# Vision-transformer tower on one core: the transfers of the extra pixel columns are issued by ScalarE instead of SyncE

## The chip, the cores and the metric

The kernel runs on one core of a Trainium2 chip. The metric is the device time of one execution in microseconds (us). A core has TensorE (PE, matrix products and transposes), VectorE (DVE), ScalarE (ACT), GpSimd (POOL) and SyncE (SP), each working through its own list of instructions in order, and 16 DMA engines that move data between memory and on-chip buffers. A transfer is started by an instruction in the list of SP, ACT or POOL. The five lists meet only through semaphores.

## The reference, cut to what matters

```
patches = X.reshape(B, C, 8, 28, 8, 28).transpose(0, 2, 4, 1, 3, 5).reshape(B, 64, 2352)   # X: (128, 3, 224, 224)
tokens  = einsum('bpi,hi->bph', patches, W) + b                      # hidden size 128
h = concatenate([class token, tokens]) * pos_embed                   # 65 tokens for each of 128 images
h = h + attention(layernorm(h))       # gated attention with an exponential moving average (4 filters) as side branch
h = h + ffn(layernorm(h))             # 8 experts, the 1024 best tokens each, gelu, scatter-add
```

The attention layer runs along the images: for one token position the 128 images are the sequence. All of it is float32. The image tensor is 77 MB and is read once.

## The kernel before, in words

**Patch products.** A patch has 3 x 28 x 28 pixels. The kernel puts channel and pixel row on the partitions (`ROWS` = 84) and takes one matrix product for each pixel column. To need fewer products, the last 9 of the 28 pixel columns (`REST`) are laid, in part, on 42 spare partitions (`EXTRA`), so that 18 products work on 126 partitions and one on 84: 19 passes (`PASSES`) for 512 columns of output.

**Chunks.** The images come in chunks of 16 images for one row of patches: 64 chunks, 8 for each row, 4 for each half of the images. A chunk n goes through these steps:
- SP: three loads (`load_chunk`, line 417) from memory into one of three raw buffers (`RING`).
- ACT: stage `C k 0`, `C k 1`, `C k 2` (line 793): three copies of pixel columns from the raw buffer into the planes that TensorE reads.
- POOL: stage `C k 3` (line 576): a copy of the last 9 pixel columns into one of two staging buffers `ST`, at the end of which `staged` is raised. It first waits until the transfers of chunk n-2 have left that buffer (`extras`).
- SP: stage `w k` (line 429, `stage_w`): waits for `staged` and issues two transfers, from 42 partitions of `ST` each to the 42 spare partitions of the planes; their landing raises `extras`.
- SP: stage `W k` (lines 437 to 439): waits for `copied` and `staged`, that is until the raw buffer is free, and issues the three loads of chunk n+3.
- PE: `token_pass` (line 1325). The first pass of a half waits for `copied` and `extras` of the half's four chunks.

**Groups and slots.** The attention works on groups of four token positions. Time is cut into slots; in each the stages of two groups (`a` the younger, `b` the older) and the work on four chunks are woven together in the one order of the list `SLOT`. Every engine walks through that list and executes those stages that it has, in that order. `run(eng, stages)` does this. A part of the list, as written in the kernel:

```python
"w 2", "C 2 1", "L b", "C 2 2", "W 2", "C 3 0", "c a", "Y b", "C 3 3", "w 3", "C 3 1", "d a", "F a", "M b",
"D a", "I a", "C 3 2", "W 3", "v a", "Q b", "R b", "K 1"]
```

The stages that matter here: `T` transposes new tokens (PE line 1356), `P`, `H`, `L`, `F`, `D`, `I`, `Q`, `R` are evaluated by ACT, mostly out of PSUM (`P` line 680 into QKT, `H` line 761, `L` line 680 into O, `F` line 709, `D` lines 716 and 720, `I` lines 725 to 738). `L b` is followed by `Y b` (DVE statistics, then two POOL instructions, lines 500 and 502), and in POOL's list `C 3 3` stands right behind `Y b`. `F a` finishes the filter output ET, and PE's stage `D` (line 1391) reads it. PE puts its token passes between the stages in fixed numbers (`FILL`): 5 after `L`, 1 after `D`, 4 after `I`, 1 after `Q`, and 4 after `T`, which are the first of a half.

There are 15 slots with chunk work. The rest of the kernel, from about 600 us on, holds the last groups, the choice of the tokens of each expert and the experts.

Of the kernel before, what the change touches and what calls it, by code (L numbers as in the profile page):

```python
# [17 lines left out]
def begun(n):  # L18

    return not isinstance(n, int) or n >= 0  # L20
# [15 lines left out]
def vit_tower(nc, x, tok_w, tok_b, cls_token, pos_embed, proj_v_w, proj_v_b, proj_mx_w, proj_mx_b,  # L36
# [10 lines left out]
    B, C, IMG, _ = x.shape  # L47
    SEQ, D = pos_embed.shape
# [5 lines left out]
    HEADS = damping.shape[1]  # L54
    MAXPOS = (rel_pos_w.shape[0] + 1) // 2
    E, _, FF = w1.shape
    FC = FF // 128
    CAP = 1024
# [14 lines left out]
    ROWS = C * PATCH  # L73
    EXTRA = ROWS // 2
    KROWS = ROWS + EXTRA
# [5 lines left out]
    CHUNKS = B // CHUNK  # L81
    CCOL = CHUNK * NP
# [6 lines left out]
    with ctx:  # L89
        def sb(name, shape, dt=F32):  # L90
            return ctx.enter_context(nc.sbuf_tensor(name, shape, dt))

        def count(name, per=1):
            return Count(ctx.enter_context(nc.semaphore(name)), per)
# [6 lines left out]
        ST = flat[:, 2 * PLANEW:2 * PLANEW + STAGEW]\  # L101
# [22 lines left out]
        X = sb("X", [128, 4, D])  # L124
# [47 lines left out]
        def area(rows, half, a, m0=0, m1=NCOL // 2):  # L172
            if a < 2:
                v = PL[rows, half, AREA * a:AREA * a + AREA].rearrange("p (m j r) -> p m j r", j=REST, r=2)
            else:
                v = PL[rows, half, 2 * AREA:PLANEW].rearrange("p (m j r) -> p m j r", j=1, r=2)
            return v[:, m0:m1]
# [98 lines left out]
        pe_pro = count("pe_pro")  # L276
# [6 lines left out]
        staged = count("staged")  # L283
        extras = [count(f"extras{a}", 32) for a in range(2)]
        pe_tok = [count(f"pe_tok{h}") for h in range(2)]
# [62 lines left out]
        def group(row, u):  # L348
            g = 2 * row + 1 + u
            return Group(row, g, u, 4, 4 * g - 3, 1 - u)  # L350
# [8 lines left out]
        def slot(i, u, a, b, tokens, more):  # L359


            keep = []
            for entry in SLOT:
                s, *w = entry.split()
                if s == "K":
                    if tokens and u == 1:
                        keep.append((s, (int(w[0]), i)))
                elif s in "CWw":
                    n = int(w[0])
                    row, half = (i, 1) if u == 0 else (i + 1, 0)  # L370
                    if tokens and (more or u == 0):
                        keep.append((s, (4 * half + n, *(int(v) for v in w[1:]), row)))
                else:
                    gr = a if w[0] == "a" else b
                    if gr:
                        keep.append((s, (gr,)))
            return keep
# [3 lines left out]
        def run(eng, stages, tokens_at=None, last=True):  # L381

            def iteration(i, slots, tokens, more):
                for u, (a, b) in enumerate(slots):
                    for s, w in slot(i, u, a, b, tokens, more):
                        if s in stages:
                            stages[s](*w)
                        if tokens_at and tokens and s not in "KCWw":
                            tokens_at(s, i, a, u)
                    if tokens_at and tokens:  # L390
                        tokens_at("end", i, a, u)

            def pair(i):
                return (group(i - 1, 0), group(i - 2, 1)), (group(i - 1, 1), group(i - 1, 0))
            iteration(0, ((CLS, None), (None, None)), True, True)
            iteration(1, ((group(0, 0), CLS), (group(0, 1), group(0, 0))), True, True)
            for i in range(2, NP - 1):
                iteration(i, pair(i), True, True)
            iteration(NP - 1, pair(NP - 1), True, False)
            if last:  # L400
                iteration(NP, pair(NP), False, False)
                iteration(NP, ((None, group(NP - 1, 1)),), False, False)


        @block.sync
        def _(sp):
            def rows_of(k, hy, c):
                return x[CHUNK * k:CHUNK * k + CHUNK, c, ds(hy * PATCH, PATCH), :].rearrange("b p w -> p b w")

            def raw(n, c):  # L410
                return RAW[PATCH * c:PATCH * c + PATCH, n % RING, :].rearrange("p (b w) -> p b w", b=CHUNK)

            def load_chunk(n):

                if n < CHUNKS * NP:
                    for c in range(C):
                        sp.dma_start(raw(n, c), rows_of(n % CHUNKS, n // CHUNKS, c)).then_inc(load[n % RING].sem, 16)  # L417

            def stage_w(k, hy):

                n = CHUNKS * hy + k
                m0 = CCOL // 2 * (k % 4)
                sp.wait_ge(*staged.done(n))
                if k % 4 == 0 and begun(hy - 1):
                    sp.wait_ge(*pe_tok[k // 4].done(hy - 1))
                if k == 4 and hy == 0:
                    sp.wait_ge(*pe_pro.done(7))
                for a in range(2):
                    sp.dma_start(area(slice(ROWS, KROWS), k // 4, a, m0, m0 + CCOL // 2),  # L429
                                 ST[EXTRA * a:EXTRA * a + EXTRA, n % 2, :, :, :]).then_inc(extras[n % 2].sem, 16)  # L430

            def stage_W(k, hy):

                n = CHUNKS * hy + k
                sp.wait_ge(*copied.done(n))
                sp.wait_ge(*staged.done(n))
                sp.sem_inc(passed_sp.sem, 1)
                load_chunk(n + RING)

            load_chunk(0)  # L440
            sp.dma_start(WN, tok_w).then_inc(w_loaded.sem, 16)
            for n in range(1, RING):
                load_chunk(n)
            for k in range(4):
                stage_w(k, 0)
                stage_W(k, 0)

            def stage_M(gr):
                sp.wait_ge(*dve_M.done(gr.g, 3))
                sp.dma_start(out[:, ds(gr.position, gr.tiles), :], O[:, 0:gr.tiles, :]).then_inc(out_stored.sem, 16)  # L450

            def stage_R(gr):
                sp.wait_ge(*dve_Q.done(gr.g))
                sp.sem_inc(passed_sp.sem, 1)
                sp.dma_start(rows_v[:, ds(gr.position, gr.tiles), 0:D], XR[:, 0:gr.tiles, :]).then_inc(row_stored.sem, 16)

            run(sp, {"w": stage_w, "W": stage_W, "M": stage_M, "R": stage_R}, last=False)


            def load_experts(h, e):  # L460
                sp.dma_start(W1s[:, h, :], w1[ds(e, 1), :, :].rearrange("e d f -> d (e f)")).then_inc(w_in[h].sem, 16)
                sp.dma_start(W2s[:, h, :, :], w2[ds(e, 1), :, :].rearrange("e (c f) d -> f (e c) d", f=128))\
                    .then_inc(w_in[h].sem, 16)

            sp.wait_ge(*pe_tok[0].done(NP - 1))
            sp.wait_ge(*pe_tok[1].done(NP - 1))
            for h in range(2):
                load_experts(h, h)
            for gr in (group(NP - 2, 1), group(NP - 1, 0), group(NP - 1, 1)):
                stage_M(gr)  # L470
                stage_R(gr)


            sp.wait_ge(*pr_ready.done(0))
            sp.dma_start(rows_v[:, :, D:ROW], PR).then_inc(pr_stored.sem, 16)

            for e in range(1, E - 1):
                sp.wait_ge(*pe_y.done(2 * e - 1))
                load_experts(1 - e % 2, e + 1)

            sp.wait_ge(*out_stored.done(LAST))
            sp.wait_ge(*row_stored.done(LAST))
            sp.wait_ge(*pr_stored.done(0))
# [150 lines left out]
        def _(act):  # L634
# [147 lines left out]
            def stage_C(k, piece, hy):  # L782
# [13 lines left out]
                if piece == C - 1:  # L796
                    ins.then_inc(copied.sem, 1)

            for k in range(4):
                for piece in range(C):  # L800
                    stage_C(k, piece, 0)
            run(act, {"C": stage_C, "T": stage_T, "X": stage_X, "E": stage_E, "F": stage_F, "D": stage_D, "I": stage_I,
                      "U": stage_U, "P": stage_P, "H": stage_H, "L": stage_L, "Q": stage_Q, "R": stage_R})


# [803 lines left out]
```

## Time and profile before

| | |
|---|---|
| median of 3 runs | 1052.44 us (1049.9 to 1062.08) |
| the profiled execution, its own time | 1068.15 us |
| its span in the profile | 1066.4 us |
| busy: PE, DVE, ACT, POOL | 754.7, 556.6, 445.9, 397.9 us |
| DMA | 126.31 MB, mean 118 GB/s |
| packets of SP's queue | 116.05 MB, 54.1% of 16 engines' span |
| mean granted TensorE clock | 0.868 |

Busy time is the time in which an engine's instructions ran. The span is from the first to the last instruction of the profiled execution; that execution was slower than the three timed ones. In the page's 40 slices of 26.7 us, the DMA engines are at nine tenths or more of their time up to about 600 us, and far below after that.

### The profile page before, as it was taken

How to read it: one execution, taken by the hardware profiler on the slowest of the kernel's cores; microseconds unless marked ns; L12 is line 12 of the kernel's file. 1: busy time of each engine (PE TensorE's matmuls, PEld its weight loads, DVE VectorE, ACT ScalarE, POOL GpSimd, SP SyncE). 2: the span in 40 equal slices, each digit the busy share in tenths (PEclk: the TensorE clock that was granted, in tenths of full speed). 3: DMA queues.
4: the chain of work that ended last, by engine and by line, in shares of the span. 5: the costliest groups of instructions: out<-in, count | busy, mean ns of one | idle time of the engine just before them, and what ended most of it. 6: DMA issues, size and time to landing. Idle time of an engine off the chain costs nothing.

```text
span 1066.4 us, 9698 instructions
## 1 busy us (share of the span) xinstructions
PE 754.7 (71%) x2872; PEld 405.2 (38%) x2872; DVE 556.6 (52%) x1238; ACT 445.9 (42%) x729; POOL 397.9 (37%) x358
## 2 busy tenths in 40 slices
PE   1155497998879989989999995533214897777950
PEld 0122244444434534544445453422213544444520
DVE  0210155776676757768877777673778232221210
ACT  0534254665655646656666532321450332121410
POOL 1021223333233333323433322171103436677775
PEclk9998898999999989999999998856555698888985
DMA  9699988999999998999999211000010113333332
GB/s 219 129 187 191 186 174 172 195 176 187 184 181 179 196 191 164 192 196 195 194 199 202 69 32 38 10 20 10 11 9 22 32 49 56 54 58 61 58 35 25
DMA packets 134625, 126.31 MB, mean 118 GB/s; under 512 B 16565, under 2 KB 124973, under 8 KB 134445
## 3 DMA queue, kind: packets, MB, share of 16 engines
q1 hardware_dynamic: 120768, 116.05, 54.1%
q0 software_dynamic: 11264, 8.66, 6.3%
q10 hardware_dynamic: 2540, 0.99, 0.5%
q8 instruction: 23, 0.38, 0.2%
q14 instruction: 30, 0.24, 0.1%
HBM read 87.92 MB, written 12.98 MB: 95 GB/s over the span
## 4 chain that ended last, share of the span: by engine, by line
PE 20%; DMA 18%; DVE 17%; POOL 15%; issue 14%; SPq 10%; ACT 4%; ACTq 1%; DVEq 0%; POOLq 0%
DMA XS<-XS 14%; POOL out L616 9%; PE bank L1325 8%; SPq L417 6%; POOL XS L605 4%; SPq L429 4%; DVE Y L949 3%; PE bank L1423 3%; DVE QT L1024 2%; ACT XS L811 2%; DVE stats L899 1%; PE bank L1531 1%; DVE XR L891 1%; DVE ET L955 1%; DMA XS<-in_x 1%
## 5 line engine op out<-in xcount | busy, mean ns | idle before, releaser
L1325 PE MATMUL bank<-XS,WT 126*128 126x512 f32 (+1 forms) x608 | 321.5, 665 | 83.7 <-DMA XS<-XS 83.7
L793 ACT ACTIVATE XS<-XS 84x1152 f32<-84x1152 f32 (+1 forms) x192 | 187.8, 1028 | 40.0 <-DMA XS<-in_x 38.4
L1325 PEld LDWEIGHTS bank<-XS,WT 126*128 126x128 f32 (+1 forms) x608 | 116.1, 200 | 226.5 <-issue 225.8
L576 POOL COPY XS<-XS 84x1152 f32<-84x1152 f32 x64 | 88.9, 1389 | 117.0 <-DMA XS<-XS 99.3
L616 POOL DMA_INDIRECT out<-XS x64 | 100.3, 1567 | 24.7 <-issue 18.6
L605 POOL DMA_INDIRECT XS<-token_rows,XS x64 | 62.2, 972 | 100.5 <-DVE XS L1222 76.0
L949 DVE TENSOR_TENSOR_SCAN Y<-qdec,XT 128x512 f32<-128x512 f32 (+1 forms) x68 | 77.4, 1159 | 12.1 <-ACT XT L680 12.1
L836 ACT ACTIVATE XS<-bank,VT 128x512 f32<-128x512 f32 x64 | 44.0, 688 | 93.8 <-PE bank L1531 68.0
L552 POOL TENSOR_TENSOR QT<-QT,XT 128x512 f32<-128x512 f32 (+1 forms) x17 | 23.7, 1397 | 124.2 <-ACT QT L761 124.2
L1010 DVE SCALAR_TENSOR_TENSOR G<-bank,VT,GT 128x512 f32<-128x512 f32 (+1 forms) x34 | 24.5, 727 | 79.9 <-PE bank L1423 79.4
L955 DVE SCALAR_TENSOR_TENSOR ET<-Y,ema_c,ET 128x512 f32<-128x512 f32 (+1 forms) x68 | 63.6, 935 | 1.8
L1531 PE MATMUL bank<-XS 128*128 128x512 f32 x128 | 64.1, 646 | 0.0
L1541 PE MATMUL bank<-XS 128*128 128x512 f32 x128 | 62.1, 631 | 0.0
L1247 DVE TENSOR_TENSOR XS<-bank,XS 128x512 f32<-128x512 f32 x16 | 11.1, 692 | 90.9 <-PE bank L1550 49.4
L1504 PE MATMUL bank<-XS 128*32 128x64 bf16 x520 | 27.9, 211 | 37.1 <-issue 21.0
L911 DVE SCALAR_TENSOR_TENSOR tokT<-bank,VT 128x512 f32<-128x512 f32 x16 | 17.7, 1104 | 55.0 <-PE bank L1325 55.0
L500 POOL TENSOR_SCALAR rsB<-mvB 128x4 f32<-128x4 f32 (+1 forms) x17 | 14.9, 876 | 80.2 <-DVE mvB L904 80.2
L891 DVE TENSOR_SCALAR XR<-O,mvC,rsC 128x128 f32<-128x128 f32 x65 | 38.5, 854 | 7.7 <-POOL rsC L502 7.7
L500 POOL TENSOR_SCALAR rsA<-mvA 128x4 f32<-128x4 f32 (+1 forms) x17 | 4.0, 233 | 102.7 <-DVE mvA L904 102.6
L680 ACT ACTIVATE XS<-bank 128x512 f32<-128x512 f32 x16 | 9.5, 594 | 74.8 <-PE bank L1522 74.8
L1504 PEld LDWEIGHTS bank<-XS 128*32 128x32 bf16 x520 | 22.4, 108 | 46.0 <-issue 29.9
L891 DVE TENSOR_SCALAR O<-O,mvB,rsB 128x128 f32<-128x128 f32 x65 | 30.3, 528 | 16.1 <-POOL rsB L502 16.1
(228 smaller groups left out, 1269.1 us busy)
## 6 DMA issues: line engine op xcount, KB each, us to landing
XS<-in_x SPq DMA_DIRECT2D x192, 392.0 KB
XS<-XS SPq DMA_DIRECT2D x128, 189.0 KB
out<-O SPq DMA_DIRECT2D x16, 256.0 KB, 10.2
token_rows<-XR SPq DMA_DIRECT2D x16, 256.0 KB, 11.6
XS<-in_L_ffn_W SPq DMA_DIRECT2D x16, 256.0 KB, 3.2
XS<-in_L_tok_W SPq DMA_DIRECT2D x1, 1176.0 KB, 10.1
XS<-token_rows,XS POOLq DMA_INDIRECT x64
out<-XS POOLq DMA_INDIRECT x64
```

Source lines behind the costliest of these rows:

```text
L417: sp.dma_start(raw(n, c), rows_of(n % CHUNKS, n // CHUNKS, c)).then_inc(load[n % RING].sem, 16)
L576: pool.tensor_copy(ST[0:ROWS, n % 2, :, :, :].rearrange("p m j r -> p m r j"), px[:, :, :, PASSES:PATCH])\
L605: pool.indirect_dma_start(out=XG[h][:, k, :], out_offset=None, in_=rows_d, in_offset=bass.IndirectOffsetOnAxis(ap=IDX[:, e, k:k + 1], axis ...
L616: pool.indirect_dma_start(out=out_flat, in_=OW[:, e % 2, k, :], in_offset=None, out_offset=bass.IndirectOffsetOnAxis(ap=IDX[:, e, k:k + 1] ...
L793: ins = act.activation(area(slice(0, ROWS), k // 4, piece, m0, m0 + CCOL // 2).rearrange("p m j r -> p m r j"), px[:, :, :, REST * piece:m ...
L891: last = dve.tensor_scalar(dst(t), src(t), mv[:, gr.parity, t, 0:1], rs[:, gr.parity, t:t + 1], ALU.subtract, ALU.mult)
L949: dve.tensor_tensor_scan(Y[:, h % 2, 0:n], qdec[:, h, 0:n], XT[:, p, 0:n], 0.0, ALU.mult, ALU.add)\
L955: dve.scalar_tensor_tensor(out=ET[:, gr.parity, 0:n], in0=Y[:, h % 2, 0:n], scalar=ema_c[:, h:h + 1], in1=ET[:, gr.parity, 0:n], op0=ALU.m ...
L1325: ins = pe.matmul(TOK[half][:, :], WT[rows, t, :], area(rows, half, t // REST)[:, :, t % REST, :], start=(t == 0), stop=(t == PASSES - 1))
L1504: last = pe.matmul(bank[0][0:32, 0:64], OHh[:, e % 2, s // 2, :, s % 2], OHn[:, e % 2, :, s // 2, :, s % 2], start=(s == 0), stop=(s == SE ...
L1531: pe.matmul(bank[3 + f][:, :], W1s[:, h, 128 * f:128 * f + 128], XGT[:, half, :], start=True, stop=True).then_inc(pe_hid.sem, 1)
L1541: last = pe.matmul(bank[7][:, :], W2s[:, h, f, :], HT[:, half, f, :], start=(f == 0), stop=(f == FC - 1))
```

## The change

`stage_w` leaves SP's list and enters ACT's. Its waits, its two transfers and its semaphores stay as they are, as does the list `SLOT`: ACT meets `w k` where SP met it. Four stages `w` that SP executed before its walk through the list, in turns with `W`, are now executed by ACT in turns with its copies.

```diff
@@ SP
-            def stage_w(k, hy):
-                n = CHUNKS * hy + k
-                m0 = CCOL // 2 * (k % 4)
-                sp.wait_ge(*staged.done(n))
-                if k % 4 == 0 and begun(hy - 1):
-                    sp.wait_ge(*pe_tok[k // 4].done(hy - 1))
-                if k == 4 and hy == 0:
-                    sp.wait_ge(*pe_pro.done(7))
-                for a in range(2):
-                    sp.dma_start(area(slice(ROWS, KROWS), k // 4, a, m0, m0 + CCOL // 2),
-                                 ST[EXTRA * a:EXTRA * a + EXTRA, n % 2, :, :, :]).then_inc(extras[n % 2].sem, 16)
...
             for k in range(4):
-                stage_w(k, 0)
                 stage_W(k, 0)
...
-            run(sp, {"w": stage_w, "W": stage_W, "M": stage_M, "R": stage_R}, last=False)
+            run(sp, {"W": stage_W, "M": stage_M, "R": stage_R}, last=False)
@@ ACT
+            def stage_w(k, hy):
+                n = CHUNKS * hy + k
+                m0 = CCOL // 2 * (k % 4)
+                act.wait_ge(*staged.done(n))
+                if k % 4 == 0 and begun(hy - 1):
+                    act.wait_ge(*pe_tok[k // 4].done(hy - 1))
+                if k == 4 and hy == 0:
+                    act.wait_ge(*pe_pro.done(7))
+                for a in range(2):
+                    act.dma_start(area(slice(ROWS, KROWS), k // 4, a, m0, m0 + CCOL // 2),
+                                 ST[EXTRA * a:EXTRA * a + EXTRA, n % 2, :, :, :]).then_inc(extras[n % 2].sem, 16)
             for k in range(4):
                 for piece in range(C):
                     stage_C(k, piece, 0)
-            run(act, {"C": stage_C, "T": stage_T, ...
+                stage_w(k, 0)
+            run(act, {"C": stage_C, "w": stage_w, "T": stage_T, ...
```

## Rows read from the trace of the kernel before

**Rows 1.** The page, slices of 26.7 us; then groups of instructions by line.

```profile
PE   1155497998879989989999995533214897777950
DMA  9699988999999998999999211000010113333332
L1325 PE MATMUL bank<-XS,WT 126*128 126x512 f32 (+1 forms) x608 | 321.5, 665 | 83.7 <-DMA XS<-XS 83.7
```

**Rows 2.** Chain of waits in order: start us, length us, what; start of a half.

```profile
120.95 11.82 DMA XS<-XS
...
168.65 6.42 PE bank L1325 x8
...
574.26 4.07 PE bank L1325 x8
```

**Rows 3.** The same chain, from the slot at 319 us to the one at 394 us.

```profile
319.44 6.16 PE bank L1325 x8
...
343.02 1.29 POOL XS L576
...
344.33 0.79 SPq L429
...
345.17 10.71 DMA XS<-XS
...
356.12 4.07 PE bank L1325 x8
...
377.07 2.51 SPq L417
...
379.62 2.10 SPq L429
...
381.77 12.07 DMA XS<-XS
```

**Rows 4.** Timeline of ACT: start, length, line, what, [idle before, releaser].

```profile
372.37 0.60 ACT L680 ACTIVATE O<-bank 128x512 f32<-128x512 f32 x1 [2.49 <-PE bank L1440]
372.87 0.47 ACT L793 ACTIVATE XS<-XS 84x128 f32<-84x128 f32 x1
373.92 2.53 ACT L793 ACTIVATE XS<-XS 84x1152 f32<-84x1152 f32 x2 [0.59 <-DMA XS<-in_x]
376.79 0.63 ACT L709 ACTIVATE ET<-ET 128x512 f32<-128x512 f32 x1 [0.34 <-DVE ET L955]
```

**Rows 5.** Timeline of POOL in the same slot.

```profile
368.59 1.77 POOL L576 COPY XS<-XS 84x1152 f32<-84x1152 f32 x1
375.05 0.93 POOL L500 TENSOR_SCALAR rsB<-mvB 128x4 f32<-128x4 f32 x1 [4.70 <-DVE mvB L904]
377.61 1.28 POOL L576 COPY XS<-XS 84x1152 f32<-84x1152 f32 x1
```

**Rows 6.** Timeline of PE: stage D and the end of stage T, twice.

```profile
377.47 1.13 PE L1391 MATMUL bank<-ET,WmT 128*128 128x512 f32 x2 [0.34 <-ACT ET L709]
...
388.99 0.60 PE L1356 MATMUL bank<-ident,tokT 128*128 128x128 f32 x4
...
607.56 4.00 PE L1325 MATMUL bank<-XS,WT 126*128 126x512 f32 x8
```

**Rows 7.** Busy time by stretch; the last three columns are granted clock, DMA share, GB/s.

```profile
314.00:316.00 2.00, 0.69 (x7) 0.45 (x5) 1.68 (x4) 1.58 (x3) 0.00 (x0) 1.00 0.99 189
316.00:318.00 2.00, 0.00 (x0) 0.00 (x0) 1.41 (x9) 2.00 (x9) 0.72 (x2) 0.84 0.88 252
322.00:324.00 2.00, 2.00 (x4) 0.82 (x3) 0.00 (x0) 0.00 (x0) 0.28 (x1) 0.50 1.00 167
...
527.10:562.90 35.80, 33.46 (x115) 17.04 (x114) 27.70 (x59) 22.81 (x36) 12.96 (x12) 1.00 0.96 197
```

**Rows 8.** One line: durations of SP's issue of the moved transfers; one of ACT's issues.

```profile
L429 SPq DMA_DIRECT2D XS<-XS x128: 746/791/3780, 15.9 to 597.9; - x128
L646 ACTq DMA_DIRECT2D ema_in<-in_L_attn_damping_factor x1: 1917/1917/1917, 7.3 to 7.3; - x1
L646 ACTq DMA_DIRECT2D ema_in<-in_L_attn_ema_expansion x1: 454/454/454, 9.8 to 9.8; - x1
```

**Rows 9.** The page, transfers by issue: KB each, us from issue to landing.

```profile
XS<-in_L_ffn_W SPq DMA_DIRECT2D x16, 256.0 KB, 3.2
```

More of the change, by code:

```diff
@@ L801, in _ @@
                     stage_C(k, piece, 0)
-            run(act, {"C": stage_C, "T": stage_T, "X": stage_X, "E": stage_E, "F": stage_F, "D": stage_D, "I": stage_I,
+                stage_w(k, 0)
+            run(act, {"C": stage_C, "w": stage_w, "T": stage_T, "X": stage_X, "E": stage_E, "F": stage_F, "D": stage_D, "I": stage_I,
                       "U": stage_U, "P": stage_P, "H": stage_H, "L": stage_L, "Q": stage_Q, "R": stage_R})
```

## The prediction

> **What bounds the kernel now.** I read the page first. Up to about 600 us both TensorE and the DMA engines are in their nines, so this is the part that the change touches; behind it no chunk is moved [rows 1]. The costliest group of PE, the token passes, sat idle for 83.7 us behind the moved transfers [rows 1]. Then the chain of waits in order of time. Between the first passes of a half at 168.65 and 574.26 us lie 11 slots, so a slot is 36.87 us long [rows 2]. One slot in detail: from the first passes at 356.12 us the groups' work leads to POOL's copy `C 3 3`, which ends at 377.61 + 1.28 = 378.89 us, 22.8 us later [rows 3, 5]. SP issues `w 3`, its transfers take 10.7 to 12.1 us to land, and the next first passes start [rows 3]. From the end of `C 3 3` that second leg takes 11.8 us in one slot (344.31 to 356.12) and 15 us in the next (378.89 to 394), where SP had been held by an issue of 2.51 us for a load [rows 3]. So a slot is a cycle of two legs, 22.8 us and about 14 us, and the landing of `w 3` is most of the second.
>
> PE itself is close behind. The last chunk slot, with no loads left, shows what the cycle is without a late landing: 607.56 - 574.26 = 33.3 us [rows 2, 6]. The DMA engines are the other neighbour: 0.96 of a slot of 35.8 us is 34.4 us of transfers [rows 7].
>
> **What the change takes away.** SP no longer issues 128 transfers of 0.79 us median [rows 8]: SP is not what a slot waits for in other places, so this alone is worth nothing; the loads behind them start a little earlier, and their cover is the DMA engines' own backlog. On a queue of its own `w 3` need not stand behind loads. No row shows such a transfer on ACT's queue beside loads. The bounds are 3.2 us, a 256 KB load with the queues nearly empty [rows 9], and today's 12.1 us [rows 3]. I take about 5 us, nearer the short end since the payload of the two is alike; within a slot it will turn out not to matter.
>
> **What it adds to ACT.** In each slot ACT executes four `w`, each a wait for POOL and two issues. The price of an issue on ACT is between 0.45 us and 1.92 us, both from ACT's own queue at the start, the long one while SP was loading [rows 8]. I take 0.79 us, the median of the very same transfers on SP, so 1.6 us for a `w`, 6.4 us a slot. ACT is busy 22.8 of 36 us [rows 7], so the time is there; the order is the trouble, since ACT executes in order.
> - `w 0` to `w 2` find POOL's copy done or nearly done. `w 0` delays `P b` by about 0.5 us and `w 1` delays `H b` by about 1 us. At `w 2` ACT arrives about 370.0, POOL's `C 2 3` ends at 370.4 [rows 5] and 1 us later by the delay of `H b`, so ACT leaves at 373.0 and, after `C 2 1`, starts `L b` at 374.3 in place of 372.37 [rows 4]. PE's result is there earlier. Behind `L b` come DVE's statistics, then POOL's `Y b`, then `C 3 3`. DVE would have been busy for 0.5 us anyway. So the first leg grows by 1.5 us, to 24.3 us, and `C 3 3` ends at 380.4.
> - `w 3` is the dear one. Behind it in ACT's list stand `C 3 1` and `F a`; behind `F a`, on PE, stage `D` and everything up to the next `T`. Today `F a` starts at 376.79, before `C 3 3` has even begun [rows 4, 5]. ACT reaches `w 3` at about 376.7 us, waits until 380.4, issues until 382.0, copies `C 3 1` until 383.3, and only then does `F a`, until 383.9. PE, which had 0.34 us idle before `D` [rows 6], gets about 6 us.
> - From the start of `D` to the end of `T` PE needs 389.59 - 377.47 = 12.1 us; 12.0 us is taken for the fastest [rows 6]. So the second leg becomes 1.6 (issues) + 1.3 (`C 3 1`) + 0.65 (`F a`) + 12.0 = 15.55 us, and the landing of `w 3`, whether 3 or 12 us after 382.0, lies beside it.
>
> Cycle: 24.3 + 15.55 = 39.85 us.
>
> **The clock.** In this trace an idle stretch of PE of 4.7 us, before 319.44, is followed by a fall of the granted clock from 1.00 to 0.50, that is from 2.4 to 1.2 GHz, and it stays there past 324 us [rows 7]. The first eight pass matmuls take 6.16 us then and 4.07 us otherwise, 2.1 us more [rows 3]. An idle stretch of 6 us before every `D` should do the same each time; what follows `D` is nearly all PE. So 41.95 us for the slot, and 41.95 - 36.87 = 5.1 us over today, whose mean already holds such falls.
>
> The Trainium skill, page "DMA: Bandwidth & Descriptors", section "Issuing engines are not separate DMA queues", says that transfers started by ACT, SP or POOL run on the same 16 engines and that another issuer saves only the sequencer's time. By that rule the transfers themselves bring nothing and the sum stays at the ACT delays, which is what I forecast; no row of before can show two issuers' transfers in a slot.
>
> **The sum.** Thirteen slots (132.8 to 607.6 us) have a group `a` and a `w 3`: 13 x 5.1 = +66 us. In the filling of the pipeline, before it, no `F a` of weight is late, and the landing at 120.95 us, 11.82 us long, is on the chain [rows 2]; on a queue of its own it may shorten to 3.2 us: -8.6 us. Together +58 us. The profiled execution would then take 1068 + 58 = 1126 us; it was 1.5% above the median of the runs, so for the median 1052.4 + 58 = 1110 us.
>
> **Rivals.**
> 1. Issues on ACT are dearer, since they are held as SP's are when loads are queued (2.51 us for a load, 2.10 us for the first of `w 3` [rows 3]). The first issue of each `w` then costs 2.1 in place of 0.79 us: 1.3 x 4 = 5.2 us more a slot, all in the cycle, +68 us: about 1178 us. For it: the 1.92 us on ACT's queue [rows 8]; against: in the slots, ACT's own queue holds only these transfers.
> 2. Faster. If transfers on a second queue pass the queued loads and ACT's waits are absorbed, the late landing goes and the cycle falls towards 33.3 us, or the 34.4 us of the DMA engines: 13 x (36.87 - 34.4) = 32 us, with the 8.6 us of the start 41 us less: 1012 us. The Trainium skill, page "DMA: Bandwidth & Descriptors", section "Queues, rings and completion order", says that each DMA engine goes round the queues that have work; that is the passing itself. It decides if `F a` isn't late by more than the 2.5 us that PE now loses a slot to late landings. Against: `F a` starts within 0.34 us of its operand and PE within 0.34 us of `F a` [rows 4, 6], so there is no slack, and `C 3 3` ends 2.1 us after the start of `F a`.
> 3. No change: the clock doesn't fall, an issue on ACT costs 0.45 us, and the delay of `L b` nearly vanishes. The cycle is 39.85 - 0.7 - 1 = 38.1 us, +1.3 us a slot, and 13 x 1.3 - 8.6 = +8 us: 1060 us.
> 4. No fall of the clock alone: 13 x 3.0 - 8.6 = +30 us, 1082 us.
>
> **How the numbers follow.** Forecast 0.50, rival 1 0.17, rival 4 0.16, rival 3 0.08, rival 2 0.09. The range from 1058 to 1170 us takes in rivals 3 and 4 and most of the way to rival 1. Less than 1% (10.5 us) is what a measurement of this kernel can't tell from no change: faster 0.09, same 0.08, slower 0.83.
>
> **What would show it.** Right: ACT's waits list POOL's line 576 with 3 to 5 us in most of 15 slots; PE's largest wait in the slots is that of stage `D` for `F a`, 5 to 7 us each, and the one for the moved transfers is nearly gone; the DMA share of a slot falls to about 0.83; the clock is at 0.50 behind each `D`; first passes of halves are about 42 us apart. The forecast is wrong if `F a` still starts before `C 3 3` has ended, or if slots are under 37 us. Rival 1 shows as a median issue well over 0.79 us on ACT's queue.

## The result, and the profile after

The changed kernel takes 1122.0 us (median of 4 runs, 1119.38 to 1125.85) against 1057.26 us of the kernel before (4 runs of the same comparison): ratio 1.059, 95% interval 1.054 to 1.064. The forecast was 1110 us, range 1058 to 1170, from slots that grow by 5.1 us. The profiled execution spans 1117.9 us, against 1066.4 us before. Medians here and below are of all runs, ratios of the fast ones alone, and the profile of experiment 6 is of a slow execution, so that its slots are not compared.

The page of the changed kernel, which answers to [rows 1]: granted clock and DMA share in tenths by slices, then costliest groups (busy, mean ns | idle before, releaser), then two kinds of transfers.

```profile
PEclk9688689889989989988988989775655598888985
DMA  9799999789789789789789611000010113333433
...
L1325 PE MATMUL bank<-XS,WT 126*128 126x512 f32 (+1 forms) x608 | 317.7, 659 | 40.1 <-DMA XS<-XS 40.0
...
L1391 PE MATMUL bank<-ET,WmT 128*128 128x512 f32 (+1 forms) x34 | 33.0, 1074 | 99.6 <-ACT ET L695 99.5
...
XS<-in_x SPq DMA_DIRECT2D x192, 392.0 KB
XS<-XS ACTq DMA_DIRECT2D x128, 189.0 KB
```

The wait of PE has changed its place. Before, PE sat idle for 83.7 us ahead of its passes, behind the moved transfers, and `D` (line 1391) was no large group. Now it is idle for 99.5 us ahead of `D`, behind `F a` (ACT, line 695), and what is left behind the transfers, 40.0 us in two waits, is in the filling of the pipeline. In the 12 slots that are compared below, the first kind falls from 30.1 us to nothing and the second grows from 4.0 to 68.7 us. The DMA engines, nearly all in their nines before, show a 7 in every third slice from the 14th on.

Waits in total (us, times, longest), of ACT and of PE in the changed kernel:

```profile
ACT XS L779 <- issue: 131.6, 45, 5.5
```
```profile
PE bank L1391 <- ACT ET L695: 99.5, 16, 12.0
PE bank L1325 <- DMA XS<-XS: 40.0, 2, 25.3
```

The 131.6 us before ACT's chunk copies (line 779) are called "issue", since the activation behind a `w` waits for nothing itself: ACT's list stood in the wait for POOL and in the two issues ahead of it. So the row to read for a wait of ACT's queue is the idle time of the next activation. In the slot below it is 5.47 us behind `w 3`: 3.8 us from the end of the last copy (354.62) to the end of POOL's (358.45), then the two issues.

One slot by the chain of waits of the changed kernel, in order of time; it answers to [rows 3] and has no DMA in it:

```profile
357.19 1.26 POOL XS L562
358.48 0.76 ACTq L795
...
359.28 0.76 ACTq L795
...
361.29 0.61 ACT ET L695
...
361.95 2.08 PE bank L1391 x2
364.02 1.71 PE bank L1394 x2
...
368.88 3.84 PE bank L1325 x8
```

PE's timeline of the same slot (start, length, instructions, [idle before, releaser]), against [rows 6]: first passes, `D`, `T`, next first passes.

```profile
335.16 4.00 PE L1325 MATMUL bank<-XS,WT 126*128 126x512 f32 x8
...
361.95 2.08 PE L1391 MATMUL bank<-ET,WmT 128*128 128x512 f32 x2 [5.64 <-ACT ET L695]
...
375.74 0.60 PE L1356 MATMUL bank<-ident,tokT 128*128 128x128 f32 x4
376.17 4.00 PE L1325 MATMUL bank<-XS,WT 126*128 126x512 f32 x8
```

The slot is 376.17 - 335.16 = 41.0 us long. `D` starts after 5.64 us of idle time, and its first two matmuls take 2.08 us, not 1.13 as in [rows 6]. The granted clock of this place, in the third column from the end of each line:

```profile
356.00:358.00 2.00, 0.31 (x1) 0.00 (x0) 1.07 (x2) 0.00 (x0) 2.00 (x2) 1.00 0.88 178
358.00:360.00 2.00, 0.00 (x0) 0.00 (x0) 1.97 (x5) 0.00 (x0) 0.45 (x1) 0.97 0.96 180
360.00:362.00 2.00, 0.05 (x1) 0.05 (x1) 1.79 (x9) 1.81 (x2) 0.00 (x0) 0.50 1.03 194
364.00:366.00 2.00, 2.00 (x4) 0.83 (x3) 1.77 (x4) 0.92 (x2) 0.95 (x1) 0.50 1.01 207
```

### The profile page after: what moved, and what is told of

It is laid out like the page before. It is cut to its first block, busy times and chain, and to the rows that moved or that the text cites. A ratio compares the mean times of both kernels' runs of the same rounds, so it can differ in the third digit from the quotient of the medians.

```text
span 1117.9 us, 9698 instructions
## 1 busy us (share of the span) xinstructions
PE 770.5 (69%) x2872; PEld 410.4 (37%) x2872; DVE 558.6 (50%) x1238; ACT 445.9 (40%) x729; POOL 395.5 (35%) x358
## 4 chain that ended last, share of the span: by engine, by line
PE 27%; POOL 20%; issue 20%; DVE 12%; DMA 7%; ACT 5%; ACTq 5%; SPq 3%; POOLq 0%; DVEq 0%
PE bank L1325 9%; POOL out L602 8%; POOL XS L562 5%; DMA XS<-in_x 4%; ACTq L795 4%; POOL XS L591 3%; PE bank L1391 3%; SPq L417 3%; DVE stats L899 3%; PE bank L1394 2%; ACT XS L811 2%; PE bank L1408 2%; PE bank L1454 1%; POOL rsA L488 1%; DVE XR L891 1%
## 5 line engine op out<-in xcount | busy, mean ns | idle before, releaser
L1325 PE MATMUL bank<-XS,WT 126*128 126x512 f32 (+1 forms) x608 | 317.7, 659 | 40.1 <-DMA XS<-XS 40.0
L779 ACT ACTIVATE XS<-XS 84x1152 f32<-84x1152 f32 (+1 forms) x192 | 193.3, 1031 | 171.1 <-issue 131.6
L1391 PE MATMUL bank<-ET,WmT 128*128 128x512 f32 (+1 forms) x34 | 33.0, 1074 | 99.6 <-ACT ET L695 99.5
L985 DVE TENSOR_TENSOR S<-bank,relb 128x512 f32<-128x512 f32 (+1 forms) x17 | 11.3, 667 | 91.6 <-PE bank L1408 91.6
L1247 DVE TENSOR_TENSOR XS<-bank,XS 128x512 f32<-128x512 f32 x16 | 11.1, 692 | 90.1 <-PE bank L1550 80.4
L1391 PEld LDWEIGHTS bank<-ET,WmT 128*128 128x128 f32 x34 | 8.3, 304 | 114.3 <-ACT ET L695 114.3
L891 DVE TENSOR_SCALAR XR<-O,mvC,rsC 128x128 f32<-128x128 f32 x65 | 40.9, 891 | 8.4 <-POOL rsC L488 8.4
```

Source lines behind the costliest of these rows:

```text
L779: ins = act.activation(area(slice(0, ROWS), k // 4, piece, m0, m0 + CCOL // 2).rearrange("p m j r -> p m r j"), px[:, :, :, REST * piece:m ...
L891: last = dve.tensor_scalar(dst(t), src(t), mv[:, gr.parity, t, 0:1], rs[:, gr.parity, t:t + 1], ALU.subtract, ALU.mult)
L1325: ins = pe.matmul(TOK[half][:, :], WT[rows, t, :], area(rows, half, t // REST)[:, :, t % REST, :], start=(t == 0), stop=(t == PASSES - 1))
L1391: pe.matmul(DB0[:, 0:n], WmT[:, 1, :], et, start=True, stop=True).then_inc(pe_D.sem, 1)
```

## The experiments

Slots are measured from the first passes behind `T` on PE's timeline, over the 12 slots that end at 607.56 us in the kernel before and at 663.06 us in the changed one: 36.58 us and 41.06 us a slot (the 36.58 hold the last slot of 33.3 us). Ratios are of the timed runs to the kernel before on the same chip, whose median there is 1057.3 us for the changed kernel, 1062.2 us for experiments 1 to 4, 1060.9 us for 5 to 8 and 1061.1 us for 9 and 10.

| | median us | ratio, 95% interval | mean of 12 slots, us |
|---|---|---|---|
| changed kernel | 1122.0 | 1.059, 1.054 to 1.064 | 41.06 |
| 1: w 3 behind F a | 1055.0 | 0.989, 0.982 to 0.996 | 36.33 |
| 2: w 3 alone on SP | 1063.7 | 0.999, 0.994 to 1.003 | 36.55 |
| 3: w 3 alone on ACT | 1119.2 | 1.051, 1.044 to 1.058 | 40.74 |
| 4: ACT waits, SP issues | 1095.2 | 1.028, 1.021 to 1.035 | 38.62 |
| 5: four passes moved before D | 1104.2 | 1.044, 1.038 to 1.051 | 39.18 |
| 6: SP issues, w 3 ahead of W 2 | 1046.2 | 0.989, 0.983 to 0.995 | not compared |
| 7: POOL issues | 1051.2 | 0.993, 0.989 to 0.998 | 35.38 |
| 8: w 2 and w 3 behind | 1054.3 | 0.995, 0.991 to 0.999 | 35.54 |
| 9: as 7, loads earlier | 1051.3 | 0.993, 0.989 to 0.998 | 35.84 |
| 10: as 6, loads earlier | 1052.8 | 0.989, 0.984 to 0.994 | 35.90 |

**1. The order alone.** The theory says that ACT's place in the order costs, not the queue. So ACT keeps all 128 transfers, and one entry of the list moves.

```diff
-"C 3 3", "w 3", "C 3 1", "d a", "F a", "M b",
+"C 3 3", "C 3 1", "d a", "F a", "w 3", "M b",
```

> The changed kernel, with w 3 standing behind F a in the list of the slot, and nothing else moved; ACT still issues all 128 transfers. Theory (ACT's order: F a waits behind w 3, which waits for POOL): F a starts about 4.5 us earlier, as soon as DVE is done; w 3 now delays the two evaluations of stage D by about 1.5 us instead. PE's idle time before D falls from 5.6 us to under 1.5 us, the clock doesn't fall there, and the slot goes from 41.0 to about 35.5 us: 12 x -5.5 = -66 us against the changed kernel, median about 1050 us. Rival (a second queue slows the loads, or the 6.2 us of issues in a slot are what ACT lacks): the slot stays at 39 to 41 us, median 1100 to 1122 us.

Measured: 1055.0 us, ratio 0.989. The whole loss is gone, with one entry moved by three places. ACT's timeline in this kernel:

```profile
337.30 2.91 ACT L779 ACTIVATE XS<-XS 84x128 f32<-84x128 f32 x3
340.77 0.63 ACT L695 ACTIVATE ET<-ET 128x512 f32<-128x512 f32 x1 [0.57 <-DVE ET L955]
342.90 1.56 ACTq L795 DMA_DIRECT2D XS<-XS  x2
344.56 0.69 ACT L702 ACTIVATE QKT<-bank,VT 128x512 f32<-128x512 f32 x1 [3.16 <-issue]
```

`F a` starts when DVE is done, and `w 3` now holds the first evaluation of `D` (line 702), after which PE is idle for 0.90 us. This slot, from 319.60 to 354.58 us, takes 34.98 us, as expected. But the mean is 36.33 us. In the other slots another wait comes last; this is the next slot's chain in the same kernel:

```profile
361.04 13.68 DMA XS<-in_x
374.74 2.51 ACT XS L779 x2
377.25 0.51 ACT ET L695
```

`C 3 0` waits for its load, and that again stands ahead of `F a`. The rivals (a slower second queue, or the sum of the issues) are out: both are the same as in the changed kernel.

**2 and 3. Which of the four w.** The two halves of the change: `stage_w` stands in both lists and returns at once for the other's share. For experiment 2 (in experiment 3 the two conditions are exchanged):

```diff
@@ SP, stage_w
+                if k % 4 != 3:
+                    return
...
@@ ACT, stage_w
+                if k % 4 == 3:
+                    return
```

> The changed kernel with w 3 alone given back to SP; w 0 to w 2 stay on ACT. Theory: F a no longer waits for POOL, the idle time before D goes; the late landing of w 3 behind the loads in SP's queue comes back as the end of the slot. Slots of 36 to 37.5 us, median 1050 to 1070 us. Rival (issues on ACT cost by their number, 3 of 4 remain): three quarters of the loss stay, median about 1105 us.

> The other half: w 3 alone on ACT, w 0 to w 2 issued by SP as before. Theory: nearly the whole loss stays; only the delay of L b by w 0 to w 2, about 1.1 us a slot, goes. Slots of about 39.9 us, median about 1109 us. Rival (cost by the number of issues): a quarter of the loss stays, median about 1073 us.

Measured: 36.55 and 40.74 us a slot. With `w 3` on SP nothing is left of the loss. With `w 3` alone on ACT, 40.74 - 36.58 = 4.2 of the 4.5 us are there. One quarter of the transfers makes nine tenths of the loss of a slot. The expected 39.9 us were too low: `w 0` to `w 2` on ACT cost only 0.3 us a slot, not 1.1. A chain of experiment 2 shows the old end of the slot come back (the passes are line 1343 there):

```profile
304.79 10.90 DMA XS<-XS
...
315.94 5.56 PE bank L1343 x8
```

**4. The wait without the issues.** SP issues everything; ACT only waits where `w` stands.

```diff
@@ ACT, stage_w (SP's stays as before)
+                act.wait_ge(*staged.done(CHUNKS * hy + k))
+                return
```

> The kernel before, SP issues all transfers; but at every place of w in its list ACT waits for POOL's copy (staged) and issues nothing. It parts the wait from the issues. Theory: the wait is most of it. At w 3 the two issues of 1.56 us are gone and L b is less late: slots of about 39.0 us, median about 1095 us. If the issues were the cost, the median would stay near 1057 us.

Measured: 1095.2 us, 38.62 us a slot. Of the 4.5 us a slot the wait alone is 2.0, and the other 2.4 come when the issues follow it; these 2.4 hold the move of the transfers to ACT's queue too. The idle time before `D` is 3.6 us in every slot here, and its first two matmuls take 2.08 us: the clock falls behind this stretch as well. The chain of this kernel goes from POOL straight to `F a` (line 709) and `D` (line 1407 there):

```profile
312.33 1.27 POOL XS L576
...
314.84 0.61 ACT ET L709
...
315.49 2.08 PE bank L1407 x2
```

No engine needs `F a` to wait for that copy: it stands behind it in a list.

**5. The clock.** The changed kernel with PE's four passes behind `I` moved to stand behind `L`, so that PE works through most of its wait for `F a`.

```diff
-FILL = {"T": 4, "P": 1, "V": 3, "L": 5, "D": 1, "I": 4, "Q": 1}
+FILL = {"T": 4, "P": 1, "V": 3, "L": 9, "D": 1, "I": 0, "Q": 1}
```

> The changed kernel, with the four token passes that PE does behind stage I moved to stand behind stage L: 9 passes behind L, none behind I. F a is as late as in the changed kernel, but PE works for 3.8 us of the 5.6 us that it waits. Theory (the idle stretch costs its own length and a fall of the clock behind it): idle time before D is under 2.5 us and the granted clock doesn't fall to 0.50 there; behind I, PE waits for ACT instead, so of the moved 3.8 us only a little is won, but the 2.2 us of the clock are. Slots of 38 to 39 us in place of 41.0, median 1085 to 1098 us. Rival (the clock follows PE's share of busy time over the slot, not the stretch; or it costs nothing since PE waits anyway): slots of 40.5 to 41 us, median 1115 to 1122 us.

Measured: 39.18 us a slot, 1104.2 us. PE's timeline in this kernel:

```profile
358.51 1.12 PE L1391 MATMUL bank<-ET,WmT 128*128 128x512 f32 x2 [1.77 <-ACT ET L695]
...
366.32 1.06 PE L1454 MATMUL bank<-Wr,X 128*128 128x8 f32 x8 [1.84 <-ACT X L666]
367.23 1.38 PE L1408 MATMUL bank<-QKT,QT 128*128 128x128 f32 x8
...
369.25 4.95 PE L1325 MATMUL bank<-XS,WT 126*128 126x512 f32 x8
```

And its clock, third column from the end:

```profile
356.00:360.00 4.00, 2.23 (x6) 0.77 (x5) 3.71 (x12) 2.12 (x3) 0.97 (x2) 1.00 1.01 190
```
```profile
368.00:372.00 4.00, 4.00 (x12) 2.44 (x11) 2.82 (x12) 3.33 (x11) 0.23 (x1) 0.58 1.01 207
```

The idle time before `D` is 1.77 us, the clock stays at 1.00 and `D` takes 1.12 us again; so it is in 10 of the 12 slots. From `D` to the first passes it is 10.7 us instead of 14.2, with the four passes gone from there. But the slot is only 1.9 us shorter, just outside what was expected, and the median missed its band by 6 us: a fall of the clock still comes, now behind the wait of 1.84 us before `R`, and slows the first passes, 4.95 instead of 4.00 us. In all 12 slots the mean clock of the first 2 us of these passes is below 1.00, between 0.50 and 0.94. Filling the idle stretch moved a part of the price instead of removing it. Since the order of passes changed too, this is no clean price of the clock.

**6. The landing of w 3.** Was the end of a slot before the landing of `w 3` behind loads? SP issues everything; `w 3` stands ahead of `W 2`.

```diff
-"C 2 2", "W 2", "C 3 0", "c a", "Y b", "C 3 3", "w 3", "C 3 1",
+"C 2 2", "C 3 0", "c a", "Y b", "C 3 3", "w 3", "W 2", "C 3 1",
```

> The kernel before, SP issuing everything, but w 3 standing ahead of W 2 in the list, so that SP is not held in W 2's load issues when POOL's copy is done and one load chunk less is queued ahead of it. Theory (the second leg of the kernel before is the landing of w 3 behind loads): landings of w 3 shorten from 10.7 to 12.1 us to 7 to 9 us, slots of 35 to 36 us, median 10 to 20 us under the kernel before. Rival (the DMA engines are full, so what w 3 gains the later loads lose): slots of 36.5 to 37.5 us, no change within 1%.

Measured: ratio 0.989, 1.1% faster. So the time can be brought down without a second queue, by the place of `w 3` in SP's own list. Experiment 10 keeps this order, and its profile shows what became of the slot's end. PE's waits for the moved transfers, first in the kernel before, then in the kernel of experiment 10:

```profile
PE bank L1325 <- DMA XS<-XS: 83.7, 15, 30.3
```
```profile
PE bank L1325 <- DMA XS<-XS: 49.9, 3, 30.7
```

The three waits that are left are in the filling: no slot ends with the landing of `w 3` any more. ACT's waits for loads grow from 38.4 to 83.5 us, and `F a` behind them is late in the long slots. The landings of `w 3` themselves, expected at 7 to 9 us, were not read.

**7. Another queue, another engine.** POOL issues the transfers right behind its own copy.

```diff
@@ POOL (gone from the other lists)
+            def stage_w(k, hy):
...
+                pool.wait_ge(*staged.done(n))
...
+                for a in range(2):
+                    pool.dma_start(area(slice(ROWS, KROWS), k // 4, a, m0, m0 + CCOL // 2),
+                                 ST[EXTRA * a:EXTRA * a + EXTRA, n % 2, :, :, :]).then_inc(extras[n % 2].sem, 16)
```

> All 128 transfers issued by POOL, right behind its own copy, in place of SP or ACT. No engine then waits for another's copy. Theory (it was ACT's place in the order, not a second queue, that cost): ACT and F a are as early as in the kernel before; POOL pays some 1 to 1.6 us an issue (its indirect transfers take that), which delays Y b, M b and the copies behind: slots between 35.5 and 38 us, median 1045 to 1075 us. Rival (a second queue itself slows the slot by contention): slots of 39 us and more, median over 1085 us.

Measured: ratio 0.993, 35.38 us a slot, the shortest of all. POOL's issues cost it less than feared, and the page gives the landing that could not be seen before; the line of one issue, then the page's row:

```profile
L575 POOL DMA_DIRECT2D XS<-XS x128: 505/520/892, 11.3 to 574.6; - x128
```
```profile
XS<-XS POOLq DMA_DIRECT2D x128, 189.0 KB, 8.8
```

So a second queue is not what costs. On POOL's a transfer lands 8.8 us after its issue in the median of all 128, between 3.3 and 11.1, and not in the 5 us that I had taken for ACT's.

**8. Both late entries moved.** ACT issues; `w 2` stands behind `L b` and `w 3` behind `F a`.

```diff
-"w 2", "C 2 1", "L b", "C 2 2", "W 2", "C 3 0", "c a", "Y b", "C 3 3", "w 3", "C 3 1", "d a", "F a", "M b",
+"C 2 1", "L b", "w 2", "C 2 2", "W 2", "C 3 0", "c a", "Y b", "C 3 3", "C 3 1", "d a", "F a", "w 3", "M b",
```

> The changed kernel with w 3 behind F a and also w 2 behind L b, so that ACT's 3.1 us wait for POOL's copy of chunk 2 no longer delays L b. Theory: the cycle by way of L b and Y b shortens by another 0.8 us, to about 34.2 us, but every other slot is bound by the loads (34.4 us of transfers a slot): slots of 35.5 to 36.3 us, median 1040 to 1055 us, 1 to 2% under the kernel before. If L b's delay is no part of the cycle, the result is that of w 3 behind F a alone.

Measured: 35.54 us a slot, of which nine are between 34.6 and 35.3 us and three between 36.8 and 39.9 us; ACT waits for loads for 61.9 us in this kernel, against 38.4 us before. The slots are as expected, the time is not: 1 to 2% less than the kernel before was expected and 0.5% came. The ratio, 0.995, cannot be told from that of experiment 1.

**9 and 10. Is a late load what is left?** In the kernels of 7 and 6 ACT's last copy of chunk 0 and the loads behind it move ahead of `P b`.

```diff
-"C 0 1", "w 0", "Z b", "P b", "C 0 2", "W 0", "N a",
+"C 0 1", "w 0", "C 0 2", "W 0", "Z b", "P b", "N a",
```

> POOL issues the moved transfers, as in the run before with that, and C 0 2 and W 0 stand ahead of P b in the list, so that ACT's last copy of chunk 0 and SP's loads behind it no longer wait for PE's transposes of P (about 1 us earlier). Theory (what is left of the slots over 34.4 us is a load that is issued too late for C 3 0): the slots of 36 to 38 us become shorter by 1 to 2 us, median 1035 to 1048 us, about 1% under the run with C 0 2 in its old place. Rival (the DMA engines are full, so an earlier issue only lengthens the landing): slots stay at 34 to 38 us, mean 35.5 us, no change within 0.5%.

> The same move of C 0 2 and W 0 in the kernel in which SP issues everything with w 3 ahead of W 2 (ratio 0.989 to the kernel before). Theory: another 0.5 to 1% faster, ratio 0.980 to 0.985. Rival (the DMA engines are full): ratio unchanged at 0.989.

Measured: 0.993 and 0.989, as without the move: the rival holds. SP's first loads of a slot are indeed issued earlier in 9 than in 7, 4.5 instead of 5.6 us behind the first passes. But the loads that the chain of waits goes through in these slots take 13.2 to 15.8 us to land, 14.1 in the mean, against 12.0 to 14.2 us, 13.2 in the mean, in 7. The stretch from 170 to 580 us in the kernel of 9 has a DMA share of 0.96:

```profile
170.00:580.00 410.00, 377.87 (x1268) 190.78 (x1267) 311.29 (x665) 254.12 (x397) 207.57 (x233) 0.98 0.96 192
```

Issued 1.1 us earlier, a load took 0.9 us longer to land. Eight of the 12 slots of 9 take 33.9 to 34.5 us and four 37.4 to 40.9 us, and the mean stays near 36. All versions that are faster than the kernel before by 0.5 to 1.1% end here, and none is told apart from the next by these intervals.

## Why the prediction was right

**The mechanism** was right in its place and its kind. `F a` is late behind `w 3`, which waits for POOL. I had PE idle for about 6 us before `D`; the trace has 5.64 us, and 5.6 to 6.5 us in all 12 slots. The wait of ACT for POOL was taken at 3.7 us and is 3.8 us. The DMA share of the slot fell to 0.85, where about 0.83 was said. Experiments 1 to 3 show that the place of `w 3` in the list is the cause, and 4 parts it into wait and issues.

**The cycle** was 41.95 us forecast and 41.0 measured. First leg: 358.45 - 335.16 = 23.3 us (forecast 24.3, before 22.8). Second leg: 376.17 - 358.45 = 17.7 us (forecast 15.55 + 2.1 = 17.65). The first leg's growth was mis-sized: 0.5 us, not 1.5. The two delays at its start are the terms that were too long. `P b` was to be 0.5 us late behind `w 0` and is not late: it starts 4.55 us after the first passes in both kernels. `H b` was to be 1 us late behind `w 1` and is 0.35 us late, 10.66 instead of 10.31 us. So ACT leaves `w 2` 16.0 us after the first passes, not 16.9. What makes `w 0` free can be seen in the changed kernel: its two issues run in ACT's queue while the activations of `U b` still run, and before the copy `C 0 1`, which stands ahead of it in the list and starts at 337.93.

```profile
336.37 0.40 ACT L733 ACTIVATE S<-S,nmax 128x128 f32<-128x128 f32 x1 [0.41 <-DVE nmax L991]
336.46 0.76 ACTq L795 DMA_DIRECT2D XS<-XS  x1
336.68 0.19 ACT L733 ACTIVATION_READ_ACCUMULATOR S<-S,nmax 128x1 f32 x1
...
337.25 0.76 ACTq L795 DMA_DIRECT2D XS<-XS  x1
...
337.93 1.31 ACT L779 ACTIVATE XS<-XS 84x1152 f32<-84x1152 f32 x1
```

**The price of an issue** was right: 0.761 us in the median on ACT's queue, where 0.79 was taken. Rival 1, dearer issues under load, did not come.

```profile
L795 ACTq DMA_DIRECT2D XS<-XS x128: 758/761/1659, 32.7 to 646.3; - x128
```

**The clock** fell behind each stretch of 5.6 us and more, to 0.50 at `D` in all 13 slots, and `D` to first passes took 14.2 us where I had 12.0 + 2.1. Rival 4, no fall, did not come.

**The thirteen slots.** From the slot that begins at 133.02 us before, and at 129.27 us in the changed kernel, to the end of the last one, the kernel before takes 607.56 - 133.02 = 474.5 us and the changed one 663.06 - 129.27 = 533.8 us: +59.3 us, or 4.6 us a slot, where 13 x 5.1 = 66 us was forecast. The changed slot was forecast 0.9 us too long (41.95 against 41.06, most of it the first leg), about 12 us in 13 slots. Against that the slot before was taken at 36.87 us, the mean of 11 slots; the mean of these 13 is 36.50 us, since the last takes 33.3, and that gives back 5 us.

**The gain at the start** is the term that was most mis-sized: -8.6 us was forecast, and the first of the thirteen slots begins 133.02 - 129.27 = 3.8 us earlier. The chain of the changed kernel in the filling:

```profile
66.42 15.75 DMA XS<-in_x
...
99.30 17.78 DMA XS<-in_x
...
119.44 9.59 DMA XS<-XS
```

`w 3` lands in 9.59 us, against 11.82 [rows 2], not in 3.2: the DMA engines are busy for 0.93 of the stretch from 30 to 160 us. Ahead of it the chain goes through two loads that take 15.75 and 17.78 us to land; before, it went through one, of 14.44 us, and then through SP's issues. I had priced one transfer on empty queues in a stretch where they are nearly always busy. By the rule cited from the Trainium skill, page "DMA: Bandwidth & Descriptors", section "Issuing engines are not separate DMA queues", another issuer saves only the sequencer's time, so no bandwidth was to be won. The traces agree as far as they go: from 170 to 580 us the DMA share is 0.95 both in the kernel before (188 GB/s) and in that of experiment 7 (193 GB/s, 3% more in slots that are 3% shorter). The single landing is a little shorter on another queue, 9.59 us on ACT's and 8.8 us in the median on POOL's, against 10.5 to 13.3 us for `w 3` at the ends of the slots on SP's.

**The sum.** By the spans the change costs 51.5 us: 59.3 - 3.8 = 55.5 by the end of the last chunk slot, less 4.0 us in the rest of the kernel, where nothing was changed and which I did not follow. By the timed runs it costs 64.7 us. The forecast of 58 us lies between them; that it fits better than its terms is in part luck. Up to the end of the last chunk slot it is 58 against 55.5 us, since slots that were forecast 7 us too dear in all stood against a gain at the start of which 4.8 of 8.6 us did not come.

## What to carry to other kernels

Before a transfer is moved to another engine's queue, look at what stands behind it in that engine's list, and when the producer that it waits for is done; a wait in a compute engine's list makes everything behind it a consumer of that producer. Here one transfer pair in four made nine tenths of the loss, and moving one entry of the order by three places gave it all back. And where the DMA engines are busy for 0.95 of the time, as here, little is to be won: a second queue brought 0.7% (experiment 7), another place in SP's list 1.1% (6), and loads issued 1.1 us earlier nothing that these intervals show (9, 10). Price landings from rows of the same load, never from an empty stretch.

## What the runs showed of the hardware beyond that

An issue on ACT's queue runs beside the activations ahead of it when its wait is already met: those of `w 0` start at 336.46 and 337.25 us, between activations of `U b`, and ahead of a copy at 337.93 us that stands before them in the list. So issues cost ACT less than their count times 0.76 us. POOL's issue of the same transfer takes 0.52 us where SP's takes 0.79 and ACT's 0.76. And in experiment 5 the wait of 1.77 us was followed by a granted clock of 1.00, and the one of 1.84 us, 6 us later, by one of 0.58; idle stretches far shorter than the 4.7 us of the kernel before can stand ahead of a fall. The length of the stretch alone does not decide it: in another slot of the same trace one of 1.80 us before `D`, at 278.80 us, was followed by a clock of 0.61 over 2 us.
